# Bands of the heads as two fp32r parts, roots at stage ends, the gate's load ahead, narrower buffers

## The chip, the cores and the metric

The kernel runs on one core of a Trainium2 chip (trn2). What is measured is the device time of one execution in microseconds. The core has TensorE (PE, matmuls; its weight loads are listed as PEld), VectorE (DVE), ScalarE (ACT), GpSimd (POOL) and SyncE (SP, which issues DMAs), each with its own queue in which instructions go in order; 16 DMA engines move data between HBM and SBUF. Engines wait for one another by semaphores.

## The reference

A stack of six blocks on x of shape (4, 1024, 256), each behind a layer norm:

```python
x = x + 0.5 * moe(norm(x))            # 16 experts, grouped top-4, two shared
x = x + attention(norm(x))            # one head of 256, softmax over 1024
x = x + 0.5 * moe(norm(x))
x = x + 0.5 * linear(norm(x))         # x and weight quantized to fp6 (e2m3), blocks of 32
x = x + heads(norm(x))                # 16 heads of 16, causal, with a bias by distance
x = x + 0.5 * linear(norm(x))
```

The heads block, which most of the change touches:

```python
xn = layernorm(x, gamma, beta)
scores = einsum('bhid,bhjd->bhij', q / 4, k) + rel[:, clip(i - j, 0, 128)]
scores = where(i >= j, scores, -inf)
y = einsum('bhij,bhjd->bhid', softmax(scores), v)
x = x0 + y @ Wo.T
```

## The kernel before

x stays in SBUF for the whole run as 32 tiles of 128 rows. The stages run one after the other: mixture of experts, attention, mixture of experts, linear (with `HeadTables` and `HeadProjection` beside it), heads, linear. `end_of_stage` (L149) lets every engine drain and then wait for all of them. Within a stage a list of steps, `order`, is written out by hand, and each engine walks the same list and issues its part of each step; an engine that waits holds back what it has in later steps.

The roots of the layer norms are taken by `act_root` on ScalarE (L171) between `dve_variance` and `dve_rsqrt` on VectorE. ScalarE loads a table of functions ahead of a root if another table is in.

The first stage, `moe(fresh=True)`: SyncE issues x of batch 0, then (`moe_order`) x of batches 1 to 3, the gate's weights (`load_gate`, L438), three weight slices (`load`), and further slices as their staging buffers come free. `split_gate` (L528 on ScalarE, L490 on GpSimd) stands ahead of the first `stat`, `root` and `norm`. Weights are split in an upper and a lower fp32r part, and a product is made of three matmuls (`three`, L126 to L128, and L782 to L784).

The linear stage (`linear`) works in quads of four tiles through some ten elementwise steps on VectorE (L1449 to L1488), with `centre`, `power` and `turn` on ScalarE. Transposed data are kept in `xts`, XTS = 3 pairs. The weight goes through the same steps first, in a buffer of its own, `wraw`. Beside it `HeadTables` builds the bias bands: for each pair of heads one matmul flips a slice (L1702), ScalarE copies it to `full` (L1678), then the band is split in three bf16 parts, `band`, by copies on ScalarE (L1689) and subtractions on GpSimd (L1668), and its transpose goes to `band_q` (L1693). `HeadProjection` makes q, k, v of batch 0.

The heads stage has 16 units (4 batches by 4 groups of 4 heads). For each unit the row maxima come first, ahead by a unit and a half: matmuls L2255, maxima on VectorE (L2172, L2181, L2184). Then `attend` goes through 12 cells of keys by queries, and in each through the four heads. A `score` is one bf16 matmul (L2275). In 9 of the 12 cells a band has to be added: 256 columns wide in six of them, 128 in three. For the first head of a cell VectorE adds it (L2210), for the other three TensorE does, with three matmuls of the bf16 identity by the band's parts (L2279). ScalarE takes the exp into `pt` (L2136); scores have three banks, so the score of a fourth head waits for the exp of the first. `value` (L2296) multiplies by v, a plain f32 product. `heads_order` puts maxima beside the scores, and two more streams: `tail`, the end of the unit before (`y_turn` L2306, and after the last unit of a batch `yt_turn` L2314, `yd` by L2152, and the output product `wo` L2324), one step at each score; and `proj`, the projection of the next batch, one step at each third score of the batch's first two units, what is left at the end of the second. A projected block of q or k is cut into three bf16 parts in `parts` (L1837, L1869, L1840, L1804) and copied to HBM (`qk_scr`, L1775), from where 12 DMAs for each unit (`load`, L1787) bring the stacks of a unit into SBUF; the load of unit u + 3 is issued at the end of unit u. `parts` is used again two projection steps later, and ScalarE waits for the copy.

## Time and profile before

| | us |
|---|---|
| median of 3 runs | 2594.3 (2590.67 to 2595.55) |
| the profiled execution | 2591.8, span 2590.0 |
| PE busy, share of the span | 2149.2 (83%) |
| DVE busy | 1546.5 (60%) |
| ACT busy | 981.1 (38%) |
| POOL busy | 324.9 (13%) |
| chain that ended last | PE 65%, DVE 22%, ACT 5%, issue 4%, DMA 3% |
| stages in the span | moe to 554, attention to 910, moe to 1445, linear to 1662, heads to 2462, linear to the end |

Busy times come from one profiled execution, and a matmul's end is modelled, so that matmuls overlap in the rows; the distance between two starts tells what one costs in a stream. A row of the timeline has the start in us from the span's start, the duration of the row in us, engine, line, operation, output and inputs, shapes, count, and in brackets the engine's idle time before it with what ended it. A row of groups has busy us, mean ns of one, and the idle time before them with its releasers.

### The profile page before, as it was taken

Reading aid. Unit: us, or ns where it says so; the run is one execution under the profiler, and the core shown is the slowest. Engines: PE = TensorE matmul, PEld = TensorE weight load, DVE = VectorE, ACT = ScalarE, POOL = GpSimd, SP = SyncE. Lnnn points to the kernel's source line nnn. Section 1 sums busy time; section 2 is a strip of 40 time slices with the busy share of each in tenths; the row PEclk is TensorE's granted clock in tenths of the full one; section 3 lists DMA queues with packets and bytes.
Section 4 is the critical chain, followed back from the end, with each engine's and each line's share of the span. In section 5 each row is a group of like instructions: output and inputs, shape, how many; then the busy total and the mean of one; then the engine's idle time right before and its main releaser. Section 6 shows DMA issues by size and latency. Waiting matters only on the chain.

```text
span 2590.0 us, 39553 instructions
## 1 busy us (share of the span) xinstructions
PE 2149.2 (83%) x13274; PEld 1578.6 (61%) x13274; DVE 1546.5 (60%) x4452; ACT 981.1 (38%) x1972; POOL 324.9 (13%) x306
## 2 busy tenths in 40 slices
PE   4489999967999955899999347578998998999846
PEld 2378888855788834788888235334454454444445
DVE  6744443446455567443443598676875875878286
ACT  4222332222333342232233234235555555555532
POOL 4230000031000044100000432311011011000000
PEclk8699999978999977999999666679999999999956
DMA  7120011110000031101110210522323323321001
GB/s 244 40 78 24 27 29 30 30 60 29 1 1 1 1 114 55 52 27 30 30 30 26 79 54 25 82 42 51 51 38 63 49 40 64 51 28 26 2 25 49
DMA packets 84040, 114.89 MB, mean 44 GB/s; under 512 B 12212, under 2 KB 73816, under 8 KB 80728
## 3 DMA queue, kind: packets, MB, share of 16 engines
q1 hardware_dynamic: 77416, 94.80, 16.8%
q0 software_dynamic: 6432, 17.57, 2.1%
q8 instruction: 116, 1.90, 0.3%
q14 instruction: 76, 0.62, 0.1%
HBM read 69.16 MB, written 43.17 MB: 43 GB/s over the span
## 4 chain that ended last, share of the span: by engine, by line
PE 65%; DVE 22%; ACT 5%; issue 4%; DMA 3%; POOL 1%; SPq 0%; ACTq 0%; DVEq 0%; POOLq 0%
PE psum L782 10%; PE psum L784 10%; PE psum L783 9%; PE psum L126 5%; PE psum L2296 5%; PE psum L127 4%; PE psum L128 4%; PE psum L2275 4%; PE psum L2255 3%; PE psum L869 3%; PE psum L2279 3%; DVE junk L2184 2%; DVE stats L159 2%; DVE m L2172 1%; DVE xn L184 1%
## 5 line engine op out<-in xcount | busy, mean ns | idle before, releaser
L2136 ACT ACTIVATE pt<-psum 128x512 f32<-128x512 f32 (+3 forms) x768 | 338.6, 492 | 272.0 <-DVE psum L2210 184.3
L747 DVE SCALAR_TENSOR_TENSOR h<-psum,xg,sg 128x128 f32<-128x128 f32 x592 | 166.9, 344 | 415.4 <-PE psum L869 415.3
L556 ACT ACTIVATE sg<-psum 128x512 f32<-128x512 f32 x180 | 107.5, 597 | 573.3 <-PE psum L784 573.3
L782 PE MATMUL psum<-w_hi,xt_hi 128*128 (+1 forms) x720 | 285.9, 397 | 32.3 <-DVE xt_lo L712 32.3
L783 PE MATMUL psum<-w_lo,xt_hi 128*128 (+1 forms) x720 | 284.1, 395 | 0.0
L784 PE MATMUL psum<-w_hi,xt_lo 128*128 (+1 forms) x720 | 283.9, 394 | 0.0
L2255 PE MATMUL psum<-ks,qs 96*128 96x512 bf16 (+3 forms) x768 | 233.8, 343 | 43.7 <-DVE m L2172 13.0
L2275 PE MATMUL psum<-qs,ks 99*128 99x512 bf16 (+3 forms) x768 | 237.8, 333 | 17.7 <-ACT pt L2136 10.8
L782 PE MATMUL psum<-w_hi,ht_hi 128*128 (+1 forms) x720 | 219.3, 305 | 0.2
L2184 DVE CUSTOM_DVE_ANT_0 junk<-psum,band_q 128x256 bf16<-128x256 f32 (+1 forms) x512 | 204.3, 399 | 22.1 <-PE psum L2255 12.2
L784 PE MATMUL psum<-w_hi,ht_lo 128*128 (+1 forms) x720 | 205.0, 285 | 0.0
L783 PE MATMUL psum<-w_lo,ht_hi 128*128 (+1 forms) x720 | 203.8, 283 | 0.0
L2279 PE MATMUL psum<-band,identb 128*128 128x256 bf16 (+1 forms) x1296 | 189.7, 256 | 0.0
L2172 DVE TENSOR_REDUCE m<-psum 128x1 f32<-128x512 f32 (+1 forms) x256 | 167.1, 653 | 31.5 <-PE psum L2255 26.9
L2275 PEld LDWEIGHTS psum<-qs,ks 99*128 99x128 bf16 x768 | 68.8, 97 | 186.0 <-ACT pt L2136 117.5
L782 PEld LDWEIGHTS psum<-w_hi,xt_hi 128*128 128x128 f32 x720 | 136.9, 190 | 58.4 <-issue 35.1
L2296 PE MATMUL psum<-pt,v 128*17 128x512 f32 (+3 forms) x1536 | 162.4, 496 | 0.0
L784 PEld LDWEIGHTS psum<-w_hi,xt_lo 128*128 128x128 f32 x720 | 136.6, 190 | 30.0
L783 PEld LDWEIGHTS psum<-w_lo,xt_hi 128*128 128x128 f32 x720 | 137.1, 190 | 22.8
L2255 PEld LDWEIGHTS psum<-ks,qs 96*128 96x128 bf16 x768 | 73.6, 98 | 119.1 <-DVE m L2184 49.7
L2279 PEld LDWEIGHTS psum<-band,identb 128*128 128x128 bf16 x1296 | 117.7, 98 | 46.6 <-issue 2.1
L869 PE MATMUL psum<-ident,h 128*128 128x128 f32 x720 | 110.1, 276 | 35.2 <-DVE ht_lo L753 35.2
(295 smaller groups left out, 4485.5 us busy)
## 6 DMA issues: line engine op xcount, KB each, us to landing
xg<-w_dram SPq DMA_DIRECT2D x54, 256.0 KB, 3.3
qk_scr<-parts SPq DMA_DIRECT2D x32, 384.0 KB, 2.6
qs<-qk_scr SPq DMA_DIRECT2D x96, 128.0 KB, 7.0
ks<-qk_scr SPq DMA_DIRECT2D x96, 128.0 KB, 7.6
xg<-rows_in SPq DMA_DIRECT2D x74, 132.0 KB, 2.2
rows_out<-yb SPq DMA_DIRECT2D x74, 128.0 KB, 1.7
x<-x_dram SPq DMA_DIRECT2D x4, 1024.0 KB, 9.6
out_dram<-x SPq DMA_DIRECT2D x4, 1024.0 KB, 4.4
```

The costliest lines, as they stand in the source:

```text
L747: ins = dve.scalar_tensor_tensor(out=h[i % 2][:, e, :], in0=u[:, e, :], scalar=xg[j % XSLOT][:, at:at + 1], in1=sg[i % 2][:, e, :], op0=AL ...
L782: pe.matmul(out, a[0], b[0], start=first, stop=False)
L783: pe.matmul(out, a[0], b[1], start=False, stop=False)
L784: return pe.matmul(out, a[1], b[0], start=False, stop=last)
L869: ins = pe.transpose(h_bank[:, e * P:(e + 1) * P], h[i % 2][:, e, :], ident[:, :])
L2136: act.activation(pt[n % NPT][:, 0:q1 - q0], st_bank(n)[:, 0:q1 - q0], ACT.Exp).then_inc(*exped.up())
L2172: dve.tensor_reduce(m3[u % 2][:, h * BT + t, 0:1], mx_ring.bank((kind, i))[:, 0:cut], AXIS.X, ALU.max).then_inc(*far_max.up())
L2184: dve.tensor_tensor_reduce(junk[:, 0:bw], bank[:, far - cut:w - cut], band_q[:, u % NHG * HG + h, 2 * P - bw:2 * P], 1.0, LOWEST, ALU.add, ...
L2255: pe.matmul(bank[:, 0:c1 - c0], qs[r][0:KS_ROWS, h, t * P:(t + 1) * P], ks[r][0:KS_ROWS, h, c0:c1], start=True, stop=True).then_inc(*(far_ ...
L2275: ins = pe.matmul(bank[:, 0:q1 - q0], ks[r][:, h, j * P:(j + 1) * P], qs[r][:, h, q0:q1], start=True, stop=not by_pe)
L2279: ins = pe.matmul(bank[:, 0:b1 - q0], identb[:, :], band[:, part, u % NHG, h, q0 - j * P:b1 - j * P], start=False, stop=(part == 2))
L2296: ins = pe.matmul(y_banks[c][h * MQ:h * MQ + DH + 1, q0 - c * BANK:BANK], v1[b % 2][:, j, g * HG + h, :], slot[:, 0:(c + 1) * BANK - q0], ...
```

## The change

Nine edits. (1) `band` holds two fp32r parts in place of three bf16 ones; the identity it is multiplied by is an fp32r copy, `ident_r`, made on GpSimd at the tables' `setup`; the bf16 identity goes. A band's upper part is a copy, the lower one the difference, written directly. (2) `end_of_stage` takes a root of one number on ScalarE ahead of the drain. (3) In `moe_order` the gate's load is issued ahead of x of batches 1 to 3, and the gate's split stands behind the first root. (4) XTS is 2. (5) `wraw` is the buffer of the fourth quad, and `centre` of that quad waits for the weight's transposes. (6) In `heads_order` a projection step is placed only where the tail has run out. (7) The last four `pt` buffers are 384 wide. (8) `junk` and `mt` share a buffer. (9) `yd` is the pair `rests` of the projection, with a wait on ScalarE on either side.

```diff
@@ end_of_stage
             done = S("stage_done")
+            act.activation(sd[0:1, 0:1], ident[0:1, 0:1], ACT.Sqrt)
             for e in (pe, act, dve, pool, sp):
@@ constants
-        pool.wait_ge(*S("const")(2))
-        pool.tensor_copy(identb[:, :], ident[:, :]).then_inc(*S("const").up())
-        pe.wait_ge(*S("const")(3))
+        pe.wait_ge(*S("const")(2))
@@ moe_order
-            order = [("load_x", b) for b in range(1, BATCH)] if fresh else []
-            order += [("load_gate", 0)] + [("load", m) for m in range(STAGES)] + [("split_gate", 0)]
+            order = [("load_gate", 0)] + ([("load_x", b) for b in range(1, BATCH)] if fresh else [])
+            order += [("load", m) for m in range(STAGES)]
...
                             order += [("stat", n // CB), ("root", n // CB)]
+                        if n == 0:
+                            order.append(("split_gate", 0))
                         order.append(("norm", n))
@@ linear
-        TILES, QUADS, XTS = 2, 4, 3
+        TILES, QUADS, XTS = 2, 4, 2
...
-                    wraw = sb(st, "wraw", [P, KD, D])
+                    wraw = quants[QUADS - 1].xm[:, 0:KD, :]
...
                                 act.wait_ge(*turned(2 * (c - QUADS) + 2))
+                            elif c == QUADS - 1 and not final:
+                                act.wait_ge(*w_turned(KD))
@@ HeadTables
-                self.band = sb(stack, "band", [P, 3, NHG, HP, 2 * P], BF16)
+                self.ident_r = sb(stack, "ident_r", [P, P], F32R)
+                self.band = sb(stack, "band", [P, 2, NHG, HP, 2 * P], F32R)
...
-                    yield [("part", (hp, 2))]
...
+                    pool.tensor_copy(self.ident_r[:, :], ident[:, :])
...
-                elif kind == "part" and i[1] < 2:
+                elif kind == "part" and i[1] == 1:
...
-                    pool.wait_ge(*self.part_ok(3 * hp + part + 1))
-                    pool.tensor_tensor(self.left[:, 0:n, :], now[:, 0:n, :], self.band[:, part, g, h0:h0 + n, :],
+                    pool.wait_ge(*self.part_ok(hp + 1))
+                    pool.tensor_tensor(self.band[:, 1, g, h0:h0 + n, :], self.full[:, 0:n, :],
+                                       self.band[:, 0, g, h0:h0 + n, :].bitcast(F32),
                                        ALU.subtract).then_inc(*self.left_ok.up())
...
                     act.wait_ge(*self.flipped(i + 1))
+                    if i:
+                        act.wait_ge(*self.left_ok(i))
@@ heads_order
-                    order.extend(next(tail, []))
-                    if step % 3 == 0:
+                    ending = next(tail, None)
+                    order.extend(ending or [])
+                    if step % 3 == 0 and ending is None:
                         order.extend(next(proj, []))
@@ attention_heads
-                pt = [sb(st, f"pt{i}", [P, BANK]) for i in range(NPT)]
+                pt = [sb(st, f"pt{i}", [P, BANK if i < 2 * HG else 3 * P]) for i in range(NPT)]
...
+                mt_all = sb(st, "mt", [P, P])
+                mt, junk = mt_all[0:HG * BT, :], mt_all[:, :].bitcast(BF16)
...
-                yd = sb(st, "yd", [P, KD, CH])
+                yd = ahead.rests
...
+                        if kind == "h_turn" and i >= 2 * KD * CB and i % (KD * CB) == 0:
+                            act.wait_ge(*wo_ok(2 * CB * (i // (KD * CB) - 1)))
...
                                 act.wait_ge(*wo_ok(2 * bc))
+                            act.wait_ge(*ahead.part2(2 * KD * CB * min(bc // CB + 2, BATCH)))
...
-                                for part in range(3):
-                                    ins = pe.matmul(bank[:, 0:b1 - q0], identb[:, :],
+                                for part in range(2):
+                                    ins = pe.matmul(bank[:, 0:b1 - q0], tables.ident_r[:, :],
                                                     band[:, part, u % NHG, h, q0 - j * P:b1 - j * P],
-                                                    start=False, stop=(part == 2))
+                                                    start=False, stop=(part == 1))
```

## Rows read from the trace of the kernel before

**Rows 1.** Windows by stage: us, busy of PE, PEld, DVE, ACT, POOL, clock, DMA.
```profile
1460.00:1660.00 200.00, 112.25 (x452) 85.01 (x452) 159.84 (x334) 79.50 (x153) 71.82 (x57) 0.66 0.19 52
...
1700.00:2500.00 800.00, 709.56 (x5036) 361.80 (x5036) 552.31 (x1942) 436.91 (x954) 60.75 (x61) 0.96 0.25 40
```
**Rows 2.** Groups by line and shape: the bands of the heads, and the exps.
```profile
L2279 PE MATMUL psum<-band,identb 128*128 128x256 bf16 x864 | 142.5, 274 | 0.0
...
L2279 PE MATMUL psum<-band,identb 128*128 128x128 bf16 x432 | 47.2, 219 | 0.0
...
L2136 ACT ACTIVATE pt<-psum 128x512 f32<-128x512 f32 (+3 forms) x768 | 338.6, 492 | 272.0 <-DVE psum L2210 184.3 <-PE psum L2275 44.7 <-PE psum L2279 40.4
```
**Rows 3.** Timeline, TensorE: narrow and wide band groups, four f32 transposes.
```profile
1891.72 0.33 PE L2279 MATMUL psum<-band,identb 128*128 128x128 bf16 x3
1891.89 0.38 PE L2255 MATMUL psum<-ks,qs 96*128 96x512 bf16 x1
...
2419.23 0.49 PE L2279 MATMUL psum<-band,identb 128*128 128x256 bf16 x3
2419.56 0.60 PE L2306 MATMUL psum<-ident,ys 128*128 128x128 f32 x4
2420.00 0.33 PE L2275 MATMUL psum<-qs,ks 99*128 99x384 bf16 x1
```
**Rows 4.** Timeline, TensorE: fp32r matmuls of 256 columns, then plain f32 ones.
```profile
1748.77 0.28 PE L126 MATMUL psum<-wv_hi,xt_hi 128*128 128x256 f32 x1
1748.89 0.28 PE L127 MATMUL psum<-wv_lo,xt_hi 128*128 128x256 f32 x1
...
2450.76 3.32 PEld L2324 LDWEIGHTS psum<-wo,yd 128*128 128x128 f32 x16 [1.10 <-issue]
```
**Rows 5.** Timeline, TensorE: what follows a group of bf16 bands.
```profile
1883.91 0.49 PE L2279 MATMUL psum<-band,identb 128*128 128x256 bf16 x3
1884.33 1.05 PE L2296 MATMUL psum<-pt,v 128*17 128x512 f32 x8
...
1936.38 0.49 PE L2279 MATMUL psum<-band,identb 128*128 128x256 bf16 x3
...
1936.95 0.39 PE L127 MATMUL psum<-xt_lo,wk_hi 128*128 128x512 f32 x1
1937.18 0.39 PE L128 MATMUL psum<-xt_hi,wk_lo 128*128 128x512 f32 x1
```
**Rows 6.** Timeline, TensorE: first output transpose in units 8, 10, 12 and 13.
```profile
2106.35 0.44 PE L2306 MATMUL psum<-ident,ys 128*128 128x128 f32 x2
...
2223.75 0.44 PE L2306 MATMUL psum<-ident,ys 128*128 128x128 f32 x2
...
2299.36 0.44 PE L2306 MATMUL psum<-ident,ys 128*128 128x128 f32 x2
...
2348.81 0.55 PE L2306 MATMUL psum<-ident,ys 128*128 128x128 f32 x3
```
**Rows 7.** SyncE and ScalarE by time, the chain, a DMA group: copy of parts.
```profile
1973.90 0.42 SPq L1787 DMA_DIRECT2D ks<-qk_scr  x1
...
1975.83 8.80 DMA qk_scr<-parts
...
1984.65 0.60 ACT L1837 ACTIVATE parts<-psum 128x512 bf16<-128x512 f32 x1 [4.54 <-DMA qk_scr<-parts]
...
ks<-qk_scr SPq DMA_DIRECT2D x96, 128.0 KB, 7.6
```
**Rows 8.** The chain and the timeline at the start of the kernel.
```profile
6.85 9.15 DMA gate_stage<-wg_dram
...
17.81 0.20 DVE L175 RECIPROCAL recip<-std 128x8 f32<-128x8 f32 x1 [7.01 <-ACT std L171]
```
**Rows 9.** Timeline, ScalarE: behind the attention stage, and in the last linear stage.
```profile
910.92 1.28 ACT L171 ACT_TABLE_LOAD   x1 [7.86 <-DVE var_eps L167]
...
2464.02 0.40 ACT L1389 ACTIVATE bias_hi<-bias 2x256 fp32r<-2x256 f32 x1
```

More of the change, by code:

```diff
@@ L134, in macaron @@
         ident = sb(ctx, "ident", [P, P])
-        identb = sb(ctx, "identb", [P, P], BF16)
         mv = sb(ctx, "mean_var", [P, NT, 2])
@@ L1576, in allocate @@
                 self.full = sb(stack, "band_full", [P, 2, 2 * P])
-                self.left = sb(stack, "band_left", [P, 2, 2 * P])
             def order(self):
@@ L1662, in on_pool @@
                                        ALU.subtract).then_inc(*self.t_lo.up())
-                elif kind == "part" and i[1] < 2:
+                elif kind == "part" and i[1] == 1:
                     hp, part = i
                     g, h0, n = self.heads_of(hp)
-                    now = (self.full, self.left)[part]
-                    pool.wait_ge(*self.part_ok(3 * hp + part + 1))
-                    pool.tensor_tensor(self.left[:, 0:n, :], now[:, 0:n, :], self.band[:, part, g, h0:h0 + n, :],
+                    pool.wait_ge(*self.part_ok(hp + 1))
+                    pool.tensor_tensor(self.band[:, 1, g, h0:h0 + n, :], self.full[:, 0:n, :],
+                                       self.band[:, 0, g, h0:h0 + n, :].bitcast(F32),
                                        ALU.subtract).then_inc(*self.left_ok.up())
@@ L1681, in on_act @@
                     g, h0, n = self.heads_of(hp)
-                    now = (self.full, self.left, self.left)[part]
                     if part == 0:
@@ L1686, in on_act @@
                             act.activation(self.band_dve[:, g, :], self.full[:, n, :], ACT.Copy)
-                    else:
-                        act.wait_ge(*self.left_ok(2 * hp + part))
-                    act.activation(self.band[:, part, g, h0:h0 + n, :], now[:, 0:n, :],
-                                   ACT.Copy).then_inc(*self.part_ok.up())
+                        act.activation(self.band[:, 0, g, h0:h0 + n, :], self.full[:, 0:n, :],
+                                       ACT.Copy).then_inc(*self.part_ok.up())
                     if part == 1:
@@ L2066, in attention_heads @@
                 v1.append(sb(st, "v11", [P, BT, HEADS, DH + 1]))
-                pt = [sb(st, f"pt{i}", [P, BANK]) for i in range(NPT)]
-                junk = sb(st, "junk", [P, 2 * P], BF16)
+                pt = [sb(st, f"pt{i}", [P, BANK if i < 2 * HG else 3 * P]) for i in range(NPT)]
                 m3 = [sb(st, f"m3{i}", [P, HG * BT, 3]) for i in range(2)]
                 mm = [sb(st, f"mm{i}", [P, HG * BT]) for i in range(2)]
-                mt = sb(st, "mt", [HG * BT, P])
+                mt_all = sb(st, "mt", [P, P])
+                mt, junk = mt_all[0:HG * BT, :], mt_all[:, :].bitcast(BF16)
                 mparts = sb(st, "mparts", [HG * BT, 3, P], BF16)
@@ L2150, in on_act @@
                                 act.wait_ge(*wo_ok(2 * bc))
+                            act.wait_ge(*ahead.part2(2 * KD * CB * min(bc // CB + 2, BATCH)))
                             act.wait_ge(*yt_turned(i + 1))
-                            act.activation(yd[:, k, :], mx_ring.bank((kind, i)), ACT.Copy).then_inc(*yd_ok.up())
+                            act.activation(yd[k][:, :], mx_ring.bank((kind, i)), ACT.Copy).then_inc(*yd_ok.up())
                 def on_dve():
@@ L2323, in on_pe @@
                                 for k in range(KD):
-                                    ins = pe.matmul(bank[:, t * D:(t + 1) * D], yd[:, k, tt * P:(tt + 1) * P],
+                                    ins = pe.matmul(bank[:, t * D:(t + 1) * D], yd[k][:, tt * P:(tt + 1) * P],
                                                     wo[:, k, :], start=(k == 0), stop=(k == KD - 1))
```

## Prediction

> **What bounds the kernel now.** I read the table of windows by stage first, for what each stretch is short of. In the stretch of the heads, from 1700 to 2500 us, TensorE is busy 709.56 us of 800 at a clock of 0.96, VectorE 552.31 and ScalarE 436.91; in the linear stage before it VectorE is busy 159.84 of 200 and TensorE 112.25 [rows 1]. So a part of the change that shortens TensorE's work pays in the heads and hardly before them. Second, the groups by line and shape: the bands of the heads are 864 matmuls of 256 columns and 432 of 128, and what ScalarE waits for in the heads is first VectorE's addition of the fourth head's band (184.3 us), then TensorE [rows 2]. Third, the timeline, for the distance from one start to the next: a modelled matmul duration contains its latency, so the cost in a stream is that distance, never the mean. Last, the chain of waits at the seams: the start, the stage ends, and the places where a batch is projected.
>
> **Bands: three bf16 parts to two fp32r parts.** Removed are 864 + 432 bf16 matmuls [rows 2], in 288 wide groups of three and 144 narrow ones. A wide group takes 2419.56 - 2419.23 = 0.33 us, a narrow one 1891.89 - 1891.72 = 0.17 [rows 3]. Added are two fp32r matmuls for each group. A wide fp32r matmul costs 1748.89 - 1748.77 = 0.12 us in a stream [rows 4], so a wide group takes 0.24: 288 x -0.09 = -26 us. The trace has no fp32r matmul narrower than 256 columns. From below it is bounded by the bf16 one, 0.17 / 3 = 0.057. From above by plain f32: 8 matmuls of 256 columns in 16 records take 3.32 us, so 0.42 each and 0.21 for half the columns [rows 4]. The nearest row is the f32 transpose of 128 columns, four in 2420.00 - 2419.56 = 0.44 us, 0.11 each [rows 3], where the weights are 4 bytes wide and the moving side is as narrow; I take 0.11. In 48 of the narrow groups a score of 512 columns runs before and covers the first load: 0.11 + 0.055 = 0.165, no change. In the other 96 a 128-column score (0.057) covers half of the load: 0.055 + 0.11 + 0.055 = 0.22 against 0.17, 96 x 0.05 = +5 us. TensorE's net is -21 us.
>
> Does the change of type from bf16 to fp32r cost something, 432 times? Behind a bf16 band group at 1936.38 the second fp32r matmul of the projection starts at 1936.95: 0.57 us, where 0.33 and one 512-column matmul (1937.18 - 1936.95 = 0.23) give 0.56. So nearly nothing. The value matmul, f32 with 17 columns of weights, starts 0.42 behind a group of 0.33, 0.09 too late [rows 5]; that is the other end.
>
> The Trainium skill (TensorE: Matmul & The Clock Gate, section Weight-path perf modes) speaks against this part: the fast weight load is on for 128 weights of a type other than FP32, and its section on LDWEIGHTS puts a plain load at columns / 1.2 GHz, 107 ns. By that rule wide groups are hidden and narrow ones are held by the load, and the trace agrees: 0.11 us for a narrow f32 transpose against 0.057 for a narrow bf16 matmul [rows 3]. By the page alone the same net would come out.
>
> Not all 21 us come through. Two heads units without projection take 2299.36 - 2223.75 = 75.61, 37.8 each [rows 6]; in each cell the first head goes TensorE, VectorE (band added), ScalarE (exp), and with three score banks the fourth score waits for that exp. What TensorE saves before such a wait becomes wait. VectorE, at 552 of 800, is not the bound but is queued. Of the two ends, all and nothing, I take 60%: **-13 us**.
>
> **Order of tail and projection.** Projection steps now start only when the tail of the unit before has run out. The order written out: for batches 2 and 3 they begin at step 21 of 48 in place of step 0, four query/key steps fall before the unit's end, the last four at steps 33 to 42 of the next unit, and no longer right behind the 12 stack loads issued at a unit's end. That matters: the load's last DMA is issued at 1973.90, the copy of the parts behind it needs 8.80 us, and ScalarE then stands 4.54 us for the buffer, with the exps behind it [rows 7]. In the chain this copy stands three times, once for each projected batch; this row is one of them. Size: a pair of units with tail and projection takes 2223.75 - 2106.35 = 117.4; two quiet units are 75.6, a tail adds (2348.81 - 2299.36) - 37.8 = 11.6 [rows 6], and the projection's matmuls 48 x 0.23 + 48 x 0.12 + 16 x 0.11 = 18.6 (48 of 512 columns, 48 of 256, 16 transposes). 105.8 in all, so 11.6 are stalls. I take half for batches 2 and 3 (two pairs) and a third for batch 1, whose second half alone moves (steps 12 to 21 of its second unit): 6 + 5 + 4 = 15, less 1 for the new waits below: **-14 us**, between 0 and -24.
> Queued behind the new waits: ScalarE's wait for the output matmuls ahead of a projection's first transpose holds back exps, but the tail is by then ten steps done; its wait for the parts before an output transpose refers to a batch projected two units ago. Both at nothing; without that cover each costs some exps of 0.49 [rows 2]. SyncE: the load of unit 4b waits for the last copy, now issued about at the unit's end; 12 issues at 0.42 and 7.6 to land [rows 7] give, from some 3 us behind the unit's end, 3 + 5.0 + 7.6 = 15.6 us, and the first maximum that reads it is 24 steps away, 18.9 us. It fits with 3 us to spare.
>
> **Start.** The gate's load is issued behind 4 MB of input and lands 9.15 us after 6.85, at 16.0; ScalarE waits for it, splits the gate, loads the root's table (1.28, as in rows 9) and takes the root, 1.8 us in all, and VectorE goes on at 17.81 after 7.01 us of idling [rows 8]. Now the gate is behind 1 MB, the root stands before the split, and the table is loaded while the input is on its way. VectorE has the variance at 17.81 - 7.01 = 10.80; without split and table at most 0.5 of the 1.8 is left, so it goes on by 11.3, -6.5 to -6.7. Next late are the first weights: their DMAs stand behind the gate's, landed after 16.0 and don't move, and ScalarE now wants them near 16: up to 2.5 us back, unless a later wait covers it. The three other input blocks start later by one small DMA; the second isn't read before about 17. **-6.5 us**, between -4 and -6.7.
>
> **Roots at stage ends.** Five further seams. Where attention ends, the table load stands on the path behind 7.86 us of idle ScalarE [rows 9]: **-1.3 us**. Before the last linear stage one stands too, but behind it ScalarE reads the bias, whose DMA is issued at the stage's start, and starts that at 2464.02 with no idle time before it [rows 9]; when the DMA landed isn't seen, so 0 to -1.3; I take 0, since a DMA of a few us would have landed only then. At the other seams the root is wanted late or a root was last; the added 0.2 us, or 1.5 with a table, lies beside the landing of the last rows. 0, at worst +0.5 each.
>
> **Linear stage, narrower buffers.** Per pair of heads ScalarE loses one or two copies, GpSimd one subtraction; VectorE bounds that stage [rows 1], and the tables' steps end sooner, so fewer flips stand in TensorE's queue. One copy of the identity (0.3) is added on GpSimd in front of the gathers. Two moved-data pairs in place of three: TensorE issues the matmuls that empty a pair before the transposes that refill it, so ScalarE's wait is already met. The weight's buffer shared with the fourth quad: its wait is met some ten rounds ahead. **-1 us**, between +2 and -5. The narrower exp buffers, the shared maximum buffer and the dropped bf16 identity change no wait: 0.
>
> **Sum.** -13 - 14 - 6.5 - 1.3 - 1 = -35.8. The profiled execution took 2591.8 (span 2590.0): 2556.0. The median of the runs, 2594.3, lies 2.5 above, so I forecast **2558.5**.
>
> **Rivals.** (a) The new order gives nothing: stalls move with the projection, as denser steps wait for GpSimd's parts, or the load of unit 4b comes late. For: only 3 us to spare. Against: the 8.80 us copy is tied to the loads before it. -22: 2572.
> (b) Narrow fp32r matmuls run at the plain f32 rate, 0.21 each: 144 x (0.42 - 0.17) = +36 in place of +5, at 60% +19: 2577. For: nothing narrow is in the trace. Against: the transposes.
> (c) Slower: the 4-byte weight loads are not overlapped between score and band, where operands change each time. Then a wide group costs 2 x (0.11 + 0.11) = 0.44 and a narrow one 2 x (0.11 + 0.055) = 0.33: 288 x 0.11 + 144 x 0.16 = +55, all on TensorE's queue. With -14 - 6.5 - 1.3 - 1 it ends at +32: 2626. It decides from +23 on: narrow groups at 0.33 and wide ones still at 0.33. Against: 0.12 in a stream, and the 0.57 above.
> (d) The start's gain is taken back by the weights' DMAs (+5): 2563, inside the range.
>
> **Numbers.** Forecast with (d) 0.63, (a) 0.20, (b) 0.12, (c) 0.05. The range takes the forecast with its bounds (bands to -21, order to -24) and (a) and (b): 2542 to 2580. About 0.2%, 5 us, can be told from no change. Faster 0.93, same 0.02, slower 0.05.
>
> **What would show it.** Band groups 0.24 and 0.17 to 0.22 us apart; quiet units at 36.9 to 37.1; the pair with projection at 108 to 112; no copy of parts over 4 us in the chain; VectorE's first reciprocal at 11.1 to 11.3 in place of 17.81; no table load behind the attention's end. Wrong if quiet units stay at 37.8, or TensorE waits where unit 4b's stacks are read.

## The result and the profile after

The changed kernel takes 2573.3 us, median of 4 runs (2570.5 to 2578.0), against 2594.5 for the kernel before in the same comparison (2590.7 to 2595.6): ratio 0.991, interval 0.989 to 0.993. That is 21.2 us less, where 35.8 were forecast. The profiled execution spans 2568.5 us. A second comparison, on another chip, gave 0.9905 (0.9889 to 0.9922). The prediction's range held the time, close to where its rival (a) put it, but 14 us of its sum did not come, and the experiments look for them.

First the stages of both kernels, in windows cut at TensorE's first matmul of each stage. The columns are the window in us, its length, busy us of TensorE, of its weight loads, of VectorE, ScalarE and GpSimd with counts, TensorE's clock, the DMA share and GB/s. The kernel before: first gated stage, attention, second gated stage, linear, heads, last linear stage.

```profile
0.00:575.00 575.00, 471.88 (x2819) 407.10 (x2819) 282.70 (x857) 167.67 (x332) 84.89 (x87) 0.93 0.20 62
575.00:912.00 337.00, 299.94 (x1856) 263.29 (x1856) 184.53 (x366) 106.66 (x163) 18.52 (x19) 0.95 0.03 9
912.00:1471.00 559.00, 470.85 (x2820) 405.28 (x2820) 275.78 (x776) 167.70 (x336) 85.92 (x85) 0.92 0.16 49
1471.00:1668.00 197.00, 112.17 (x452) 84.91 (x452) 156.40 (x327) 77.41 (x148) 69.81 (x53) 0.66 0.21 50
1668.00:2482.00 814.00, 719.35 (x5042) 357.43 (x5043) 567.12 (x2022) 430.65 (x942) 65.79 (x64) 0.95 0.28 43
2482.00:2590.00 108.00, 74.96 (x288) 60.57 (x286) 79.97 (x109) 31.00 (x53) 0.00 (x0) 0.64 0.12 39
```

The changed kernel, the same six:

```profile
0.00:568.00 568.00, 473.37 (x2819) 408.46 (x2819) 284.46 (x857) 166.83 (x332) 84.49 (x87) 0.93 0.20 62
568.00:904.00 336.00, 301.06 (x1856) 264.30 (x1856) 184.56 (x367) 107.41 (x165) 18.42 (x19) 0.95 0.03 9
904.00:1461.00 557.00, 469.95 (x2820) 405.37 (x2821) 277.69 (x776) 167.87 (x335) 86.18 (x86) 0.92 0.17 49
1461.00:1659.00 198.00, 119.73 (x452) 88.95 (x452) 154.42 (x326) 70.61 (x133) 63.07 (x45) 0.60 0.21 50
1659.00:2460.00 801.00, 701.40 (x4608) 374.27 (x4608) 569.49 (x2021) 425.60 (x942) 65.59 (x64) 0.95 0.28 44
2460.00:2568.00 108.00, 75.71 (x288) 61.34 (x288) 80.60 (x110) 31.84 (x55) 0.00 (x0) 0.63 0.12 39
```

The differences are -7, -1, -2, +1, -13 and 0 us. The windows are cut at whole microseconds; from first matmul to first matmul the heads take 813.3 and 801.2, 12.1 less. The start is there in full. The heads, for which -13 and -14 were forecast together, gave 12 in all. TensorE is busy 18 us less in them, where 21 were forecast, so the bands did shorten its work about as forecast; the time did not follow.

The band groups, from TensorE's timeline (start, duration, engine, line, operation, out<-in, shape, count). A score of 512 columns with its wide group, then the next matmul; further down a 128-column score with its narrow group:

```profile
2005.02 0.38 PE L2285 MATMUL psum<-qs,ks 99*128 99x512 bf16 x1
2005.05 0.59 PE L2289 MATMUL psum<-band,ident_r 128*128 128x256 f32 x2
2005.48 0.50 PE L2265 MATMUL psum<-ks,qs 96*128 96x512 bf16 x2
...
2030.38 0.22 PE L2285 MATMUL psum<-qs,ks 99*128 99x128 bf16 x1
2030.40 0.42 PE L2289 MATMUL psum<-band,ident_r 128*128 128x128 f32 x2
2030.66 0.39 PE L2265 MATMUL psum<-ks,qs 96*128 96x512 bf16 x1
```

The first score and its group take 0.46; less the 0.22 of a score of 512 columns, the group is 0.24. The second pair takes 0.28, less 0.057 about 0.22. Both are what the prediction said, against the 0.33 and 0.17 of [rows 3].

The first output transposes of units 8, 10 and 12, which answer to [rows 6]:

```profile
2086.20 0.55 PE L2316 MATMUL psum<-ident,ys 128*128 128x128 f32 x3
...
2204.73 0.55 PE L2316 MATMUL psum<-ident,ys 128*128 128x128 f32 x3
...
2279.02 0.55 PE L2316 MATMUL psum<-ident,ys 128*128 128x128 f32 x3
```

Two quiet units (units without projection) take 74.29 in place of 75.61, so 37.15 each (forecast 36.9 to 37.1, before 37.8). The pair with projection and tail takes 118.53, where 108 to 112 was forecast and the kernel before took 117.40. These rows refute a part of the prediction.

TensorE's waits from the first score of the heads on (out, waiting line, what it waited for, us in total, times, longest), the kernel before:

```profile
PE psum L2275 <- ACT pt L2136: 10.8, 31, 3.2
PE psum L2255 <- DVE rest L1869: 9.9, 6, 3.3
```

and the changed kernel:

```profile
PE psum L2285 <- ACT pt L2145: 19.0, 43, 3.2
...
PE psum L2265 <- DVE rest L1872: 3.8, 11, 0.5
```

The wait behind a late copy of the parts (9.9 us on `rest`, 3.3 at longest, [rows 7]) has indeed gone, down to 3.8 and 0.5; ScalarE, which stood 12.0 us in three waits for the copies themselves before, no longer waits for one. The wait of the scores for the exps (`pt`) has grown by 8.2 and made up for it. With the order alone (the first experiment) it is 14.7, so about half of that growth comes with the order and half with the bands.

### The profile page after: what moved, and what is told of

Same layout as the page of the kernel before. It is cut to its first block, busy times and chain, and to the rows that moved or that the text cites. A ratio compares the mean times of both kernels' runs of the same rounds, so it can differ in the third digit from the quotient of the medians.

```text
span 2568.5 us, 38687 instructions
## 1 busy us (share of the span) xinstructions
PE 2141.2 (83%) x12842; PEld 1602.7 (62%) x12842; DVE 1551.2 (60%) x4452; ACT 970.2 (38%) x1961; POOL 317.8 (12%) x298
## 4 chain that ended last, share of the span: by engine, by line
PE 61%; DVE 27%; ACT 5%; issue 4%; DMA 2%; POOL 1%; DVEq 0%; ACTq 0%; SPq 0%; POOLq 0%
PE psum L783 10%; PE psum L785 10%; PE psum L784 10%; PE psum L126 5%; PE psum L2306 4%; PE psum L127 4%; PE psum L128 4%; DVE mt L2194 3%; PE psum L2285 3%; PE psum L870 3%; DVE m L2182 2%; DVE stats L160 2%; PE psum L2265 2%; DVE m L2191 2%; DVE xn L185 2%
## 5 line engine op out<-in xcount | busy, mean ns | idle before, releaser
L2145 ACT ACTIVATE pt<-psum 128x512 f32<-128x512 f32 (+3 forms) x768 | 333.9, 493 | 274.7 <-DVE psum L2220 180.3
L2194 DVE CUSTOM_DVE_ANT_0 mt<-psum,band_q 128x256 bf16<-128x256 f32 (+1 forms) x512 | 204.1, 399 | 18.5 <-PE psum L2265 8.3
L2289 PE MATMUL psum<-band,ident_r 128*128 128x256 f32 (+1 forms) x864 | 214.9, 337 | 0.0
L2289 PEld LDWEIGHTS psum<-band,ident_r 128*128 128x128 f32 x864 | 149.8, 194 | 19.0 <-issue 0.4
```

The source lines that it names most:

```text
L2145: act.activation(pt[n % NPT][:, 0:q1 - q0], st_bank(n)[:, 0:q1 - q0], ACT.Exp).then_inc(*exped.up())
L2194: dve.tensor_tensor_reduce(junk[:, 0:bw], bank[:, far - cut:w - cut], band_q[:, u % NHG * HG + h, 2 * P - bw:2 * P], 1.0, LOWEST, ALU.add, ...
L2289: ins = pe.matmul(bank[:, 0:b1 - q0], tables.ident_r[:, :], band[:, part, u % NHG, h, q0 - j * P:b1 - j * P], start=False, stop=(part == 1))
```

## The experiments

Twelve runs were made, four to a chip; each ratio is to the kernel before on the same chip, and a saving in us is the ratio's distance from 1 times 2594.5, or the distance between two ratios. A trace is one execution of each. Where a pair is named, the second and third pair go from the first output transpose of unit 4 to that of unit 6, and of 8 to that of 10; the first pair goes from the first score of unit 0 to that of unit 2.

**The order alone.** The kernel before with

```diff
-                    order.extend(next(tail, []))
-                    if step % 3 == 0:
+                    ending = next(tail, None)
+                    order.extend(ending or [])
+                    if step % 3 == 0 and ending is None:
                         order.extend(next(proj, []))
```

> The kernel before with the new order of tail and projection alone. Theory of the prediction (the stalls go once the projection stands behind the tail and away from the stack loads): 14 us less than before, 2580, and pairs with projection at 108 to 112 in place of 117 to 120. Theory after the comparison (the projection costs 33 us beyond quiet steps in either order; the stalls only change place, from the copy of the parts to VectorE's queue of maxima and to the norm and scale steps): within 3 us of before, 2591 to 2595, pairs of units 4 and 5 and of 8 and 9 within 2 us of before.

Measured: 0.9964 (0.9951 to 0.9978), that is 9.3 us less, between 5.7 and 12.7. It is neither of the two. The three pairs of this kernel, in windows:

```profile
1736.20:1851.00 114.80, 103.64 (x680) 52.35 (x681) 84.08 (x294) 63.84 (x135) 19.46 (x17) 0.96 0.20 43
1934.88:2052.19 117.31, 105.13 (x724) 57.30 (x724) 78.91 (x269) 65.80 (x140) 19.39 (x17) 1.00 0.31 56
2127.79:2245.36 117.57, 105.14 (x725) 57.31 (x725) 78.91 (x269) 65.74 (x140) 19.38 (x17) 1.00 0.30 55
```

To compare, the kernel before, unchanged, on another chip:

> The kernel before, unchanged, for its trace on the chip on which the others run. Expected: ratio 1.000. What it tells: how long the three pairs of units with projection are here (119.6, 120.3 and 117.4 in the first trace) and how much time TensorE spends in them at the lower clock (24 us in the first trace); if the pairs vary with that time and quiet units don't, the clock after a stall is part of what a stall costs.

Measured: ratio 0.9996 (0.998 to 1.0012).

```profile
1727.20:1846.70 119.50, 106.15 (x680) 53.60 (x681) 84.02 (x294) 63.54 (x135) 19.55 (x17) 0.94 0.20 41
1930.59:2049.07 118.48, 106.68 (x724) 59.25 (x725) 75.67 (x265) 64.82 (x138) 17.14 (x16) 0.97 0.31 56
2124.67:2243.50 118.83, 106.68 (x724) 59.34 (x724) 75.81 (x265) 64.76 (x138) 17.13 (x16) 0.97 0.30 55
```

The new order gives 4.7 in the first pair, and 1.2 and 1.3 in the other two, 7.2 together. In those two the clock stands at 1.00 in place of 0.97. The prediction's own formula for the third pair, with the order alone: 117.57 - 75.6 for two quiet units - 11.6 for the tail - 18.6 for the projection's matmuls leaves 11.8 us of stalls, at full clock; for the same pair the kernel before had 11.6 in its first trace and 13.0 in its second. The projection stalls nearly as long as it did, in other places. One of them is a small cast on VectorE that takes 2.37 and 2.38 us in the second and third pair; it comes with the new order and is looked at below.

**The start alone.** The kernel before with the gate's load in front of the input and the gate's split behind the root:

```diff
-            order = [("load_x", b) for b in range(1, BATCH)] if fresh else []
-            order += [("load_gate", 0)] + [("load", m) for m in range(STAGES)] + [("split_gate", 0)]
+            order = [("load_gate", 0)] + ([("load_x", b) for b in range(1, BATCH)] if fresh else [])
+            order += [("load", m) for m in range(STAGES)]
...
+                        if n == 0:
+                            order.append(("split_gate", 0))
                         order.append(("norm", n))
```

> The kernel before with the gate's load in front of the input and the gate's split behind the root, nothing else. Theory: the first reciprocal of VectorE at 10.6 in place of 17.8, and the first stage ends 7.2 us sooner; as the gate's split also moves behind the root in the second gated stage, about 1 more there: 2586. Rival (d): the weights that load behind the gate take 5 back, 2592. If the other share of what the after kernel gains at the stage ends comes from this reordering and not from the roots, this kernel gains 9 to 10: 2584 to 2585.

Measured: 0.9989 (0.9980 to 0.9998), 2.9 us less, between 0.5 and 5.2. In its trace the first stage ends at 576.0, in that of the order alone, on the same chip, at 584.4: 8.4 less. So the traces show the start's gain in the first stage and the runs show less than half of it at the end. In the trace of this kernel the heads, in which not one instruction differs from the kernel before, take 817.5 us at a clock of 0.94, against 813.3 and 812.8 at 0.95 in the two traces of the kernel before. Whether that is the start's doing or a difference between executions, one trace can't tell. The same from the other side, the changed kernel with the start as it was:

> The changed kernel with the start as before (the gate behind the input, split ahead of the first normalisation), the roots at stage ends kept. By the traces the new start is worth 7.3 in the first stage: 0.9905 + 0.0028 = 0.9933. By the runs of the start alone, 3 us: 0.9916.

Measured: 0.992 (0.9903 to 0.9938). Against the changed kernel's 0.9905 to 0.991 that is 3 to 4 us slower, with intervals that overlap, so that 0 and 7 are possible too. On this chip the first stage ends at 575.5 with the old start and at 568.9, 569.3 and 570.4 in the three kernels with the new one. Two comparisons agree on about 3 us; where the rest is given back was not found.

**The bands alone.** The changed kernel with three bf16 parts again, made as before:

```diff
-                                for part in range(2):
-                                    ins = pe.matmul(bank[:, 0:b1 - q0], tables.ident_r[:, :],
+                                for part in range(3):
+                                    ins = pe.matmul(bank[:, 0:b1 - q0], identb[:, :],
...
```

> The after kernel with three bf16 parts for the bands again, all else as after. Theory: quiet units back from 37.1 to 37.8, 16 units by 0.66, so 10.5 us slower than after: 2584. If the type fp32r cost something elsewhere in the stream, less than 10; if the whole of TensorE's 18 us saving came through, 2591.

Measured: 0.9937 (0.9921 to 0.9952), so the two fp32r parts are worth about 0.003, 7 to 8 us, where 10.5 were expected; the intervals leave 2 to 14. Its heads take 806.3 us against the changed kernel's 801.2 and, in the trace that comes next, 798.8. The changed kernel once more, on another chip:

> The changed kernel, unchanged, beside the others on one chip. If the parts add up, it is as much faster than the three-part bf16 kernel as the quiet units say: 10 units by 0.66 and 6 units of the projection pairs by 0.66 as well would give 10.5 us; if the pairs give nothing, as in the first trace (350.2 us for the three pairs with either kind of bands), 6 to 7 us. Ratio to before 0.990 to 0.992.

Measured: 0.9905 (0.9889 to 0.9922). The second and third pair, first with bf16 parts, then as changed:

```profile
1922.38:2039.78 117.40, 105.12 (x725) 57.32 (x725) 78.92 (x269) 65.65 (x140) 19.38 (x17) 1.00 0.31 56
2115.38:2233.21 117.83, 105.12 (x725) 57.30 (x724) 78.91 (x269) 65.94 (x140) 19.39 (x17) 1.00 0.30 56
```

```profile
1912.46:2029.32 116.86, 103.38 (x670) 59.98 (x671) 78.94 (x269) 65.03 (x140) 19.46 (x17) 1.00 0.30 55
2103.58:2220.59 117.01, 103.32 (x671) 60.00 (x671) 78.94 (x269) 65.02 (x140) 19.43 (x17) 1.00 0.31 56
```

A pair of projected units gains 0.5 to 0.8 where two quiet ones gain 1.3. In the first trace of the changed kernel the same two pairs took 118.1 and 118.5, at a clock of 0.99. The same instructions, the same waits of 1.21 and 1.13 us, and in one execution the clock halves behind them, in the other not. TensorE, changed kernel, first trace:

```profile
2108.76 0.28 PE L2285 MATMUL psum<-qs,ks 99*128 99x256 bf16 x1 [1.21 <-ACT pt L2145]
...
2113.41 0.39 PE L2265 MATMUL psum<-ks,qs 96*128 96x512 bf16 x1 [1.13 <-DVE m L2182]
...
2114.35 1.88 PE L2306 MATMUL psum<-pt,v 128*17 128x512 f32 x8
```

and its second execution:

```profile
2131.73 1.05 PE L2306 MATMUL psum<-pt,v 128*17 128x512 f32 x8
```

The same eight value matmuls take 1.88 at 1.2 GHz (the window from 2114 to 2118 has 0.57) and 1.05 at 2.4 GHz. The two pairs are 1.2 and 1.5 us longer in the first execution than in the second.

**How much of TensorE's time comes through.** The changed kernel, with one matmul for each band group (the output then lacks the bands' lower part):

> The changed kernel with the second part of every band left out (its matmul, not its making; the output loses that part). TensorE has 18 x 0.12 + 9 x 0.115 = 3.2 us less a unit. Theory (half of what TensorE saves comes through, since the fourth score waits for an exp): quiet units at 35.4 to 35.6 in place of 37.1. Rival A (TensorE sets the pace, all comes through): 33.9. Rival B (ScalarE and VectorE set it by now): 36.8 to 37.1.

Measured: quiet units at (2293.12 - 2220.29) / 2 = 36.42, from the rows that answer to [rows 6]. TensorE has 3.2 us less a unit and the unit is 0.73 shorter: 23%. It is between the theory's 50% and rival B's 36.8 to 37.1, and nearer to B. The ratio, 0.9886 (0.9858 to 0.9913), is 5 us below the changed kernel's beside it, with overlapping intervals, and decides nothing more. The chain of waits suggests why. Two quiet units of the kernel before, then of the changed one (the view ends each list where it does):

```profile
by line: PE psum L2296 22.6%; PE psum L2275 18.2%; PE psum L2255 16.0%; PE psum L2279 14.0%; DVE junk L2184 8.2%; DVE m L2181 5.1%; DVE m L2172 4.5%; issue 3.8%; DVE psum L2210 3.1%; ACT pt L2136 2.6%; PE psum L2306 1.7%; DVE m L2184 0.3%; 
```

```profile
by line: PE psum L2306 19.4%; DVE mt L2194 16.7%; PE psum L2285 13.5%; DVE m L2182 11.3%; PE psum L2265 9.1%; DVE m L2191 8.9%; issue 6.4%; PE psum L2289 6.2%; DVE psum L2220 3.6%; ACT pt L2145 2.7%; PE psum L2316 1.8%; DVE m L2194 0.5%; DV
```

VectorE's maxima (`junk` and `m`, later `mt` and `m`) and its addition hold 21% of the chain before, 41% after, and 46% with one band matmul. So VectorE looks like the second bound: what TensorE saves in a unit soon turns into waiting for it. No run shortened VectorE's own work in a quiet unit, so this is read from the chain and not shown by an experiment.

**The early steps, first attempt.** The changed kernel, with

```diff
-                    if step % 3 == 0 and ending is None:
+                    if step % 3 == 0 and (ending is None or g == 0 and step < 9):
```

> The after kernel, but the norm, add and scale steps of a batch's first half stand at steps 0, 3 and 6 of the unit, ahead of the tail, as before the change; the rest waits for the tail. Theory (they cost nothing there, and 2.2 us where they stand now, because VectorE's four normalisations of 0.35 fall into its queue of maxima): 2.2 less for each of the two pairs, 4 to 5 us in all, 2569. Rival (the stall belongs to the projection as a whole and moves on to the next step): no change, 2573.

Measured: 0.9946 (0.9928 to 0.9963), some 10 us slower than the changed kernel on another chip, so both guesses missed. The pairs take 121.2 and 123.0, at clocks of 0.97 and 0.96. The early steps themselves cost next to nothing: from a unit's first score to its first output transpose it takes 7.41 us with them and 7.27 without. But every later step came forward too, and the first query/key step now falls at step 27, behind two waits (0.83 and 1.56), and runs at the lower clock (0.51 from 2142.6 to 2149.5):

```profile
2143.02 1.17 PE L2265 MATMUL psum<-ks,qs 96*128 96x512 bf16 x2 [1.56 <-DVE m L2182]
2144.13 0.80 PE L126 MATMUL psum<-xt_hi,wq_hi 128*128 128x512 f32 x1
```

**The early steps, the others kept.** The three steps of both halves of batches 2 and 3 at steps 0, 3 and 6, and nothing in the places that they leave:

```diff
-                    yield [("norm", bc)]
-                    yield [("add", bc)]
-                    yield [("scale", bc)]
+                    for kind in ("norm", "add", "scale"):
+                        yield [(kind, bc)] if b < 2 else []
...
+                    if step in (0, 3, 6) and g < 2 and 1 <= b < BATCH - 1:
+                        order.append((("norm", "add", "scale")[step // 3], (b + 1) * CB + g))
```

> The changed kernel, but norm, add and scale of both halves of batches 2 and 3 stand at steps 0, 3 and 6 of units 4, 5, 8 and 9, where the tail has not yet begun; every other projection step stays where it is. Theory (what made the kernel with early steps slow was that all later steps moved forward into step 27; the early steps themselves are free, and where they stand now they cost 2.2 and 1.8 us a half and leave two waits of over 1 us on TensorE, behind which its clock halves): 3 to 5 us less for each of the two pairs, pairs at 113 to 115, 6 to 10 us less than after in all. Rival (the steps cost the same wherever they stand): as after.

Measured: 0.9874 (0.9855 to 0.9893), against 0.9905 for the changed kernel in the same comparison: 8 us less. The two pairs:

```profile
1916.96:2031.59 114.63, 103.19 (x671) 59.92 (x671) 75.43 (x265) 63.84 (x138) 16.95 (x15) 1.00 0.30 55
2106.00:2220.70 114.70, 103.34 (x670) 59.89 (x671) 75.43 (x265) 63.84 (x138) 16.94 (x15) 1.00 0.31 57
```

So norm, add and scale cost 2.2 to 2.3 us a pair where the change put them (116.86 and 117.01, at the same clock). That is 4.5 of the 8. The rest lies outside what the edit touches: the first pair, the same in both kernels, took 115.7 at a clock of 0.93 in one trace and 113.4 at 0.97 in the other.

**Why they cost that.** VectorE and GpSimd in unit 5 of the changed kernel:

```profile
1968.73 2.37 DVE L2210 CAST mparts<-mt 32x128 bf16<-32x128 f32 x1
...
1971.46 0.21 DVE L2210 CAST mparts<-mt 32x128 bf16<-32x128 f32 x1
```

```profile
1968.56 2.36 POOL L1798 TENSOR_TENSOR x<-x,xn 128x1024 f32<-128x1024 f32 x1 [19.01 <-DVE xn L185]
```

The cast of the maxima (a copy from f32 to bf16) takes 0.21 at its next turn and 2.37 here, where GpSimd's add of the projection began 0.17 before it; it ends 0.18 behind the add. Meanwhile VectorE adds no band and takes no maximum, and the exps and scores behind it wait. In the changed kernel this happens once in each pair, in the first of them in unit 0, in the others in the second unit (2.27, 2.37 and 2.38). In the kernel before it happens in the first pair only, also for 2.27; in the others GpSimd's shorter subtraction (1.15) holds a cast for 1.04. The change moved the add of the second half of batches 2 and 3 to the steps at which the maxima are cast. In the kernel that keeps its places the 2.27 of unit 0 is the only one above 0.5. The next experiment replaced the cast by a maximum over one element:

```diff
-                            dve.tensor_copy(mparts[:, part, :], mt[:, :]).then_inc(*max_part.up())
+                            dve.tensor_reduce(mparts[:, part, :], mt[:, :].unsqueeze(2), AXIS.X,
+                                              ALU.max).then_inc(*max_part.up())
```

> The changed kernel with VectorE's three small casts of the maxima (32x128 f32 to bf16, 0.21 us) written as a maximum over one element, an instruction that copies the same values. In the changed kernel one such cast takes 2.27 to 2.38 us in each projected pair, and each time GpSimd's add of 128x1024 (2.35 us) started 0.1 to 0.2 us before it and both end together; exps and scores wait behind it. Theory (the cast is held by GpSimd's add, because both want the same port): the casts stay under 0.5 us, the waits of 3.2 and 1.2 us go, about 2 us less for each pair and less low clock behind: 5 to 8 us less than after in all, ratio 0.988. Rival (VectorE is slow there for another reason, such as the mask's DMA): the new instruction takes 2.3 us as well, and nothing moves.

Measured: 0.9881 (0.9856 to 0.9906), 6 to 8 us less than 0.9905 to 0.991, its interval overlapping theirs. VectorE and GpSimd:

```profile
1972.90 0.26 DVE L2210 TENSOR_REDUCE mparts<-mt 32x128 bf16<-32x128 f32 x1
1973.19 2.03 DVE L2215 TENSOR_TENSOR mt<-mt,mparts 32x128 f32<-32x128 f32 x1
```

```profile
1972.73 2.36 POOL L1798 TENSOR_TENSOR x<-x,xn 128x1024 f32<-128x1024 f32 x1 [19.05 <-DVE xn L185]
```

The reduction runs through the add in 0.26, and the subtraction behind it, with both inputs in SBUF, is held instead: 2.03. The theory was right about what holds the cast, and the cure was half a cure. In the second and third pair nothing is gained (118.1 and 116.8), so the ratio came out as forecast without the saving for each pair that it was made of. In the first pair an addition of a band slips in between, and the pair takes 110.40 in place of 113.4 and 115.7. The Trainium skill (SBUF — State Buffer, section Who interferes with whom) states that VectorE and GpSimd share one port pair under an exclusive lock, taken by a cast in a two-port mode and by an operation with two SBUF inputs, never by a reduction; by that rule all three rows come out as they are. What this experiment does not separate is how much of the 2.2 us a pair is the held cast and how much the normalisations that stand among VectorE's maxima.

**Out of the casts' way in the first pair too.** The kernel with places kept, and in units 0 and 1 norm, add and scale of the second half ahead of the value projections:

```diff
...
+                    if b == 1 and not c:
+                        for kind in ("norm", "add", "scale"):
+                            yield [(kind, bc + 1)]
...
```

> As the kernel that keeps its places (norm, add and scale of batches 2 and 3 at steps 0, 3 and 6), and in units 0 and 1 norm, add and scale of batch 1's second half stand ahead of the value projections, at steps 27 to 33, so that GpSimd's add is over before the casts at steps 33 to 37. Theory (the cast held for 2.27 us and the low clock behind it are what makes the first pair long): first pair at 110 to 112 in place of 113.4 to 115.7, all else as with the places kept, 2 to 4 us less than that: ratio 0.986. Rival: the stall is the projection's own and moves: ratio 0.987.

Measured: 0.9857 (0.9837 to 0.9878), median 2561.1 beside 2597.6 for the kernel before.

```profile
1701.80:1811.00 109.20, 99.90 (x626) 55.00 (x627) 81.61 (x294) 63.15 (x135) 19.39 (x17) 0.97 0.21 45
1893.86:2008.39 114.53, 103.15 (x671) 59.91 (x671) 75.43 (x265) 63.79 (x138) 16.92 (x15) 1.00 0.29 56
2082.86:2197.22 114.36, 103.25 (x670) 59.91 (x671) 75.41 (x265) 63.79 (x138) 16.91 (x15) 1.00 0.32 57
```

The first pair is 4.2 us shorter than in the better of the changed kernel's two traces (113.4 and 115.7), at the same clock of 0.97, and no cast in this kernel takes more than 0.48. The ratio alone could not tell this from the rival's 0.987; the pair does. This kernel beats both: some 37 us less than the kernel before and 12 to 14 less than the changed one.

**The roots.** The changed kernel without the root of one number at stage ends:

> The changed kernel without the roots of one number at the stage ends. Theory of the prediction: 1.3 us slower, the table load of 1.28 stands on the path again behind the attention's end and nowhere else: 0.991. If the load stands on the path at the last stage too: 2.6, 0.9915. Rival (the added root costs as much at the other seams as it saves): 0.9905.

Measured: 0.991 (0.9893 to 0.9927), too close to decide by time. The traces decide. TensorE's first matmul behind the attention, without the added root, then in the changed kernel:

```profile
910.27 1.08 PE L793 MATMUL psum<-ident,xn 128*128 128x128 f32 x4 [6.71 <-DVE xn L183]
```

```profile
906.58 0.66 PE L795 MATMUL psum<-ident,xn 128*128 128x128 f32 x2 [5.43 <-DVE xn L185]
```

It waits 6.71 us without the root, as in the kernel before, and 5.43 with it; before the last stage 21.72 and 21.24.

## Why the prediction was right and wrong

**Bands, TensorE's part: right.** Groups at 0.24 and 0.22, and a 512-column score with a narrow group unchanged. The rival with plain f32 rate (b) and the one with uncovered weight loads (c) are refuted by the rows at 2005.02 and 2030.38.

**Bands, how much comes through: too high.** The prediction took 60% for all units. Quiet units gave 0.65 of 1.3 us, 50%; the second and third pair 0.5 to 0.8 of 2.6, 20 to 30%. The term was 13; the runs give about 8. It named the wait for the fourth score's exp as what keeps the rest. That wait is there (ScalarE waits 180.3 us for VectorE's addition, 184.3 before), but the one-part kernel shows that there is more: with 3.2 us less on TensorE only 0.7 come out, and the chain has VectorE's maxima in it, of which the prediction said that VectorE "is not the bound but is queued". A busy share of 552 of 800 [rows 1] did not show how near VectorE is to the pace inside a unit; the chain of one quiet unit gives it 21% before the change, a first sign. That VectorE is the second bound is argued from these chains.

**Order of tail and projection: mis-sized, and its rule wrong.** Forecast 14, measured 9.3 by the runs of the order alone and 7.2 by its pairs. The first pair gave 4.7 for a forecast of 4. In the other two, 1.2 and 1.3 came for 5 to 6 each. The failing step is the one that finds 11.6 us of stalls and then says "I take half". It treated the copy's stall as something that only has to be removed. The copy's wait did go, as announced: ScalarE's 12.0 us in three waits are gone, no copy of parts is in the changed kernel's chain of the heads, and TensorE does not wait for the stacks of a batch's first unit. Rival (a) had the right outcome for these two pairs (the stalls move with the projection) and both of its mechanisms wrong; that its 2572 is nearest to the measured 2573.3 is luck, since the first pair did gain and the bands and the start gave less than it took. What took the stall's place is in the order itself. The first steps that wait for the tail are norm, add and scale. Before, those of a batch's first half stood at steps 0 to 6 of the unit, where they cost 0.14 us (7.41 against 7.27 up to the first output transpose). Now they stand between VectorE's maxima, and the add of the second half beside a cast, which it holds for 2.37 us. Moving them out gave 2.2 to 2.3 us a pair; the rest of the 11.8 was not taken apart. The prediction followed what each step of the projection waits for, and never asked what its GpSimd work does to VectorE. The trace of before has the same event in another place: a cast of 2.27 us in unit 0.

**The clock: left out.** The later pairs of the kernel before took 120.2 at a clock of 0.96, 118.5 and 118.8 at 0.97, and 117.4 at 0.99. The prediction took the last, the mildest, as its yardstick, and did not reckon with a stretch at half the clock behind a stall, as the rows at 2114.35 and 2143.02 show it. What the new order gives in these pairs, 1.2 and 1.3 us, comes with a clock of 1.00 in place of 0.97 and is no more than the difference between such pairs of one kernel. In the first trace of the changed kernel such pairs are 1.2 to 1.5 us longer than in the second, where these stretches are missing.

**Start: right in its place, smaller at the end.** VectorE's first reciprocal starts at 10.63 (forecast 11.1 to 11.3, before 17.81, [rows 8]), since the root waits for nothing else:

```profile
10.63 0.20 DVE L176 RECIPROCAL recip<-std 128x8 f32<-128x8 f32 x1 [0.27 <-ACT std L172]
```

The first stage is 7.2 us shorter in the first comparison, 7 to 8 and 7 to 10 on two other chips and 5 to 7 on the last, about the 6.5 or more, and rival (d) is refuted there: ScalarE waits 0.38 for the first weights and the stage keeps the gain. Yet the runs of the start alone give 2.9 with an upper end of 5.2. This stays open.

**Roots: right, and one seam more.** Attention's end gave 6.71 - 5.43 = 1.28 for a forecast of 1.3. The last stage gave 0.5 where 0 was taken and 0 to 1.3 allowed. There the root is early and the bias is now what is waited for:

```profile
2441.58 0.23 ACT L172 ACTIVATE std<-var_eps 128x32 f32<-128x32 f32 x1 [4.79 <-DVE var_eps L168]
...
2442.70 0.41 ACT L1391 ACTIVATE bias_hi<-bias 2x256 fp32r<-2x256 f32 x1 [0.69 <-DMA bias<-fb_dram]
```

So the bias landed behind the root, as supposed, and its landing hides some 0.8 of the load's 1.28.

**Linear stage: no change seen.** Forecast -1; the stage takes 197 and 198 in the two traces and 194 to 199 in others with its linear stage; a kernel with the old linear stage (the order alone) once took 203.5. Within the bound, and not resolved.

**The sum again.** Start 3, order 9, bands 8, roots 1.8: 22, where the two comparisons of the changed kernel give 21 and 25. That the sum fits does not make each term sure: the intervals above leave 3 us and more on each. Of the missing 14, some 5 belong to the order, 5 to the bands, 3 to 4 to the start and 1 to the linear stage.

## What to carry to other kernels

When steps are moved, list for each the engines it occupies and what stands on VectorE at the new place: here a GpSimd add of 2.35 us made a small VectorE cast beside it as long as itself. Take the share of a saving that comes through from the chain of one steady unit, not from busy shares; VectorE, busy for 70% of the heads, held 21% and then 41% of the chain of a quiet unit. And take a stall's price together with that of the clock behind it, from several like stretches and not from the mildest.

## What the runs showed of the hardware

A cast of 32x128, 0.21 us by itself, took 2.27 to 2.38 beside a GpSimd add of 2.35; a reduction of the same operands took 0.26 in the same spot, and a subtraction with two SBUF inputs 2.03. With the same waits on the same engines, TensorE's clock stayed at 1.00 in one execution of the changed kernel and fell to 0.57 over 4 us in another, on another chip. Two fp32r matmuls of 128 columns behind a score of 128 took 0.22, 0.11 each, as an f32 transpose of that width in [rows 3].
